# Tiled convolution: column pairs spread and further ahead, silu in halves, copies interleaved on ScalarE, a tile's rows in two parts on VectorE

## The reference

```python
f = fftshift(fft2(x))                                   # over rows and columns
amp, phase = abs(f), angle(f)
mod_amp = amp * sigmoid(amp @ w_h + b_h) + amp * sigmoid(amp @ w_l + b_l)
spatial = real(ifft2(ifftshift(mod_amp * exp(1j * phase))))
conv = conv3x3(spatial, w_f, padding='SAME') + b_f
y = silu(conv) + x
y = layernorm(y, over channels, eps=1e-3) * gamma + beta
```

## Time and profile before

| | us |
|---|---|
| runs, median (lowest to highest) | 4281.23 (4280.12 to 4282.1) |
| the profiled execution | 4282.0 |
| its span, first to last instruction | 4280.1 |
| PE busy in the span | 3983.8 (93%) |
| DVE busy | 3492.5 (82%) |
| ACT busy | 3194.4 (75%) |
| POOL busy | 2587.1 (60%) |
| start of the convolution stage of the four images (first column pair to last, L217) | 230.2 to 1654.5 |

### The profile page before, as it was taken

The page is one execution under the profiler, slowest core; times in us unless marked ns, Lnnn a source line. Parts: engine busy times, 40 slices in busy tenths (PEclk is TensorE's granted clock), DMA queues, the critical chain, the costliest instruction groups (busy, mean ns, idle before and its releaser), DMA issues.

```text
span 4280.1 us, 95150 instructions
## 1 busy us (share of the span) xinstructions
PE 3983.8 (93%) x31687; PEld 2863.5 (67%) x31687; DVE 3492.5 (82%) x8772; ACT 3194.4 (75%) x4968; POOL 2587.1 (60%) x2713
## 2 busy tenths in 40 slices
PE   7998898799979985799999999999999999999998
PEld 4787578757865885466666666666666666666665
DVE  4568447745775485699999999999999999999997
ACT  4445534553456354699999999999999999999997
POOL 0036103600460056588888888888888888888886
PEclk9999999999989998899999999999999999999999
DMA  2013101400140022111111111111111111111110
GB/s 91 1 53 129 57 2 63 156 20 11 63 164 3 11 72 81 38 41 38 42 39 42 39 42 39 42 39 42 39 39 40 39 42 39 42 39 42 39 42 26
DMA packets 214865, 205.93 MB, mean 48 GB/s; under 512 B 14368, under 2 KB 149152, under 8 KB 214688
## 3 DMA queue, kind: packets, MB, share of 16 engines
q1 hardware_dynamic: 214688, 203.60, 14.6%
HBM read 136.45 MB, written 67.11 MB: 48 GB/s over the span
## 4 chain that ended last, share of the span: by engine, by line
PE 58%; ACT 0%; DVE 0%; POOL 0%; issue 0%; POOLq 0%; DVEq 0%; ACTq 0%
PE g_ps L1043 7%; PE g_ps L1028 6%; PE g_ps L986 6%; PE g_ps L972 5%; PE g_ps L1031 5%; PE g_ps L1060 5%; PE g_ps L1003 3%; PE g_ps L1073 3%; PE g_ps L1079 3%; PE g_ps L1052 3%; PE g_ps L1012 3%; PE g_ps L977 3%; PE g_ps L992 2%; PE g_ps L1068 2%; PE g_ps L965 2%; PE g_ps L997 1%
## 5 line engine op out<-in xcount | busy, mean ns | idle before, releaser
L1355 DVE TENSOR_TENSOR g_mmat<-g_emat,g_ps 128x1024 f32<-128x1024 f32 x512 | 598.9, 1210 | 1.4 <-PE g_ps L1003 1.4
L1194 ACT ACTIVATE g_emat<-g_ps 128x1024 f32<-128x1024 f32 x512 | 521.1, 1024 | 85.7 <-PE g_ps L1031 84.2
L1298 DVE SCALAR_TENSOR_TENSOR g_acc<-g_ps,g_conv_w,g_acc 128x504 f32<-128x504 f32 (+1 forms) x768 | 554.5, 722 | 10.3 <-ACT g_acc L1157 9.9
L873 POOL TENSOR_TENSOR g_acc<-g_acc,g_tap 128x508 f32<-128x508 f32 x384 | 482.5, 1271 | 123.6 <-DVE g_acc L1298 123.6
L613 POOL MEMSET f_s_hi<- 128x192 f32 x4 | 1.0, 258 | 820.7 <-PE f_ps L344 820.7
L1043 PEld LDWEIGHTS g_ps<-g_mmat,g_dtx 128*32 128x32 f32 x8192 | 192.6, 109 | 310.6 <-issue 181.7
L1028 PE MATMUL g_ps<-g_rz,g_l 128*128 128x512 f32 x1024 | 390.0, 462 | 1.6 <-DVE g_z L1383 1.6
L229 PE MATMUL f_ps<-f_s_hi,f_wf_hi 128*128 128x256 f32 x1152 | 360.3, 313 | 5.0 <-DVE f_s_lo L466 5.0
L415 ACT ACTIVATE f_s_hi<-f_ps 128x384 fp32r<-128x384 f32 x256 | 125.7, 491 | 274.0 <-PE f_ps L217 268.9
L1043 PE MATMUL g_ps<-g_mmat,g_dtx 128*32 128x128 f32 x8192 | 329.2, 279 | 0.0
L230 PE MATMUL f_ps<-f_s_lo,f_wf_hi 128*128 128x256 f32 x1152 | 326.2, 283 | 0.0
(11 more groups left out here) (194 smaller groups left out, 12374.3 us busy)
## 6 DMA issues: line engine op xcount, KB each, us to landing
f_xt<-in_x_cols SPq DMA_DIRECT2D x32, 1024.0 KB, 10.3
f_xres<-in_x SPq DMA_DIRECT2D x128, 256.0 KB, 2.8
z<-f_zout SPq DMA_DIRECT2D x128, 256.0 KB, 2.0
g_zin<-z SPq DMA_DIRECT2D x128, 256.0 KB, 2.7
g_zres<-z SPq DMA_DIRECT2D x128, 256.0 KB, 2.9
out<-g_outb SPq DMA_DIRECT2D x128, 256.0 KB, 3.0
f_wf_raw<-in_w_f SPq DMA_DIRECT2D x1, 576.0 KB, 6.9
g_wx<-in_in_proj_t SPq DMA_DIRECT2D x1, 192.0 KB, 2.3
```

The costliest lines, as they stand in the source:

```text
L873: pool.tensor_tensor(acc[:, j, :, 1:], acc[:, j, :, 1:], tap1[:, j, :, 0:P - 1], ALU.add).then_inc(add_p[j], 1)
L1194: act.activation(emat[:, g, :].rearrange("p (b n) -> p b n", b=2), ps[:, D_BANK[g]:D_BANK[g] + 2, :], ACT.Exp).then_inc(e_a[g], 1)
L1298: dve.scalar_tensor_tensor(out=acc[:, j, :, k:], in0=four(ps[:, bank, :])[:, :, 0:P - k], scalar=conv_w[:, j, 3 - k:4 - k], in1=acc[:, j, ...
L1355: dve.tensor_tensor(mmat[:, g, :].rearrange("p (h n) -> p h n", h=HEADS), emat[:, g, :].rearrange("p (h n) -> p h n", h=HEADS), ps[:, CB, ...
```

## The change

- Seven column pairs, not five, are made ahead of tile 0 (AHEAD), in the banks 6, 7, 3, 4, 5, 0, 1. In `conv(k)` the pairs 4k+7 to 4k+10 follow the matmul groups 3, 7, 11 and 15 of 18 (a group is one shift of one position, three matmuls), so three are at least twelve matmuls apart; before they followed positions 0 to 3, nine apart.
- VectorE writes the rows without a step into a new buffer `rows_y` (a part of `work`), row by row; `tile_rows` is split. Its first part (L477 to L483) comes ahead of the last low part of the iteration, the second, `tile_ends` (L486 to L491), behind it. The first part also waits until silu of tile k-1 is done with `rows_y`.
- VectorE's iteration k is now: lo 4k+7, residual and moments (k-2, 0), lo 4k+8, residual and moments (k-2, 1), lo 4k+9, tile_rows(k), lo 4k+10, tile_ends(k).
- Silu reads `rows_y` and writes `conv_y`, two instructions of 512 elements a tile, with the step of 16 bytes now in its writes; it counts `silu_done` per half.
- ScalarE's iteration k is now: silu(k-1, 0), hi 4k+7, silu(k-1, 1), hi 4k+8, center(k-3, 0), hi 4k+9, middle(k), center(k-3, 1), hi 4k+10.
- The last three turned halves of an image use the banks 0, 1, 2 and not bank 7, and need not wait for each other's residual.

GpSimd and SP are unchanged. The core of the diff:

```diff
+AHEAD = 7
+HEAD_BANKS = (6, 7, 3, 4, 5, 0, 1)
+        rows_y = work[:, 3:5, :].rearrange("p a (b n) -> p (a b) n", b=2)
...
             def columns(b, u):
-                if u == 5:
-                    pe.wait_ge(lo_ready, b * UNITS + 1)
-                if u > 5:
-                    pe.wait_ge(lo_ready, b * UNITS + u)
-                bank = (6, 7, 3, 4, 5)[u] if u < 5 else 6
+                if u >= AHEAD:
+                    pe.wait_ge(lo_ready, b * UNITS + (1 if u == AHEAD else u))
+                bank = HEAD_BANKS[u] if u < AHEAD else 6
...
             def turn(b, k, h):
-                pe.wait_ge(silu_done, b * BATCHES + (k + 1))
-                pe.wait_ge(ysum_done, b * PARTS + (2 * k + h + 1))
+                pe.wait_ge(silu_done, b * PARTS + (2 * k + h + 1))
+                n = 2 * k + h
+                pe.wait_ge(ysum_done, b * PARTS + (min(n, 2 * BATCHES - 4) + 1))
+                bank = 7 if n <= 2 * BATCHES - 4 else n - 2 * BATCHES + 3
...
                 for n, p in enumerate((1, 3, 2, 4, 0, 5)):
-                    if n == 3 and k >= 2:
-                        turn(b, k - 2, 1)
-                    mm = position(k, p)
+                    for x in range(3):
+                        at = 3 * n + x
+                        if at == 9 and k >= 2:
+                            turn(b, k - 2, 1)
+                        mm = products(k, p, x)
+                        if at in (3, 7, 11, 15) and 4 * k + AHEAD + at // 4 < UNITS:
+                            columns(b, 4 * k + AHEAD + at // 4)
...
-                    if n < 4 and 4 * k + 5 + n < UNITS:
-                        columns(b, 4 * k + 5 + n)
...
-                def silu(k):
-                    act.wait_ge(y_done[k % 2], b * 8 + (k // 2 + 2))
-                    y = conv_y[:, k % 2].rearrange("p n i -> p (n i)")
-                    act.activation(y, y, ACT.Silu, bias=bias[:, 2:3]).then_inc(silu_done, 1)
+                def silu(k, h):
+                    if h == 0:
+                        act.wait_ge(y_done[k % 2], b * 8 + (k // 2 + 2))
+                    if k >= 2:
+                        act.wait_ge(vT_mm, b * PARTS + (2 * k - 3 + h))
+                    half = slice(4 * h * TILES, 4 * (h + 1) * TILES)
+                    act.activation(conv_y[:, k % 2, half].rearrange("p n i -> p i n"), rows_y[:, :, half], ACT.Silu,
+                                   bias=bias[:, 2:3]).then_inc(silu_done, 1)
...
                 for k in range(BATCHES + 3):
-                    for n in range(4):
-                        if 4 * k + 5 + n < UNITS:
-                            hi_part(4 * k + 5 + n)
-                        if n == 0 and 1 <= k <= BATCHES:
-                            silu(k - 1)
-                        if n in (1, 2) and k >= 3:
-                            center(k - 3, n - 1)
+                    if 1 <= k <= BATCHES:
+                        silu(k - 1, 0)
+                    if 4 * k + AHEAD < UNITS:
+                        hi_part(4 * k + AHEAD)
+                    if 1 <= k <= BATCHES:
+                        silu(k - 1, 1)
+                    if 4 * k + AHEAD + 1 < UNITS:
+                        hi_part(4 * k + AHEAD + 1)
+                    if k >= 3:
+                        center(k - 3, 0)
+                    if 4 * k + AHEAD + 2 < UNITS:
+                        hi_part(4 * k + AHEAD + 2)
                     if k < BATCHES:
                         middle(k)
+                    if k >= 3:
+                        center(k - 3, 1)
+                    if 4 * k + AHEAD + 3 < UNITS:
+                        hi_part(4 * k + AHEAD + 3)
...
                 dve.wait_ge(sum_done, done)
-                dve.scalar_tensor_tensor(out=y[:, :, 2], in0=sums[:, near], scalar=0.25, in1=sums[:, far],
+                if k:
+                    dve.wait_ge(silu_done, b * PARTS + 2 * k)
+                dve.scalar_tensor_tensor(out=rows_y[:, 2, :], in0=sums[:, near], scalar=0.25, in1=sums[:, far],
                                          op0=ALU.mult, op1=ALU.add)
...
+            def tile_ends(b, k):
...
-                dve.tensor_tensor(y[:, :, 0], ends[:, near], sums[:, far], ALU.add)
-                dve.tensor_tensor(y[:, :, 3], ends[:, far], diffs[:, far], ALU.add).then_inc(y_done[k % 2], 1)
+                dve.tensor_tensor(rows_y[:, 0, :], ends[:, near], sums[:, far], ALU.add)
+                dve.tensor_tensor(rows_y[:, 3, :], ends[:, far], diffs[:, far], ALU.add).then_inc(y_done[k % 2], 1)
...
                 for k in range(BATCHES + 2):
                     for n in range(4):
-                        if 4 * k + 5 + n < UNITS:
-                            lo_part(b, 4 * k + 5 + n)
-                        if n in (0, 2) and k >= 2:
-                            residual(b, k - 2, n // 2)
-                            moments(b, k - 2, n // 2)
+                        if n == 3 and k < BATCHES:
+                            tile_rows(b, k)
+                        if 4 * k + AHEAD + n < UNITS:
+                            lo_part(b, 4 * k + AHEAD + n)
+                        if n < 2 and k >= 2:
+                            residual(b, k - 2, n)
+                            moments(b, k - 2, n)
                     if k < BATCHES:
-                        tile_rows(b, k)
+                        tile_ends(b, k)
```

More of the change, by code:

```diff
@@ L219, in columns, with products @@
                 mm.then_inc(s_mm, 1)
-            def position(k, p):
+            def products(k, p, x):
                 at = 8 * k % RING
@@ L225, in position @@
                 out = ps[:, 3 * (k % 2) + bank, half * 256:half * 256 + 256].rearrange("p (w t) -> p w t", w=8)
[L226 to L232 removed]
+                hi = s_hi[:, at + x:at + x + 8, p * TILES:(p + 1) * TILES]
+                lo = s_lo[:, at + x:at + x + 8, p * TILES:(p + 1) * TILES]
+                pe.matmul(out, wf_hi[:, p, x, :], hi, start=(x == 0), stop=False)
+                pe.matmul(out, wf_hi[:, p, x, :], lo, start=False, stop=False)
+                return pe.matmul(out, wf_lo[:, p, x, :], hi, start=False, stop=(x == 2))
             def turn(b, k, h):
[L235 to L236 removed]
+                pe.wait_ge(silu_done, b * PARTS + (2 * k + h + 1))
+                n = 2 * k + h
+                pe.wait_ge(ysum_done, b * PARTS + (min(n, 2 * BATCHES - 4) + 1))
+                bank = 7 if n <= 2 * BATCHES - 4 else n - 2 * BATCHES + 3
                 y = conv_y[:, k % 2].rearrange("p n i -> p (n i)")
                 for r in range(4):
[L239 removed]
+                    mm = pe.transpose(ps[:, bank, r * P:(r + 1) * P], y[:, (4 * h + r) * P:(4 * h + r + 1) * P], ident[:, :])
                 mm.then_inc(vT_mm, 1)
             def conv(b, k):
[L243 removed]
+                pe.wait_ge(lo_ready, b * UNITS + (AHEAD if k == 0 else min(4 * k + 5, UNITS)))
                 pe.wait_ge(y_done[k % 2], b * 8 + (k // 2 + 1))
@@ L347, in _ @@
                     pe.wait_ge(t_free[j], b * 8 + 8)
-                for u in range(5):
+                for u in range(AHEAD):
                     columns(b, u)
@@ L409, in hi_part @@
                     act.wait_ge(s_mm, b * UNITS + (u + 1))
-                    at, bank = 2 * u % RING, (6, 7, 3, 4, 5)[u] if u < 5 else 6
+                    at, bank = 2 * u % RING, HEAD_BANKS[u] if u < AHEAD else 6
                     if at == 0 and u:
@@ L471, in tile_rows @@
                 done = b * BATCHES + (k + 1)
-                first, ends = ps[:, 3 * (k % 2), :], ps[:, 3 * (k % 2) + 2, :]
-                y = conv_y[:, k % 2]
+                first = ps[:, 3 * (k % 2), :]
                 near, far = slice(0, 256), slice(256, 512)
@@ L479, in tile_rows @@
                 dve.wait_ge(sum_done, done)
-                dve.scalar_tensor_tensor(out=y[:, :, 2], in0=sums[:, near], scalar=0.25, in1=sums[:, far],
+                if k:
+                    dve.wait_ge(silu_done, b * PARTS + 2 * k)
+                dve.scalar_tensor_tensor(out=rows_y[:, 2, :], in0=sums[:, near], scalar=0.25, in1=sums[:, far],
                                          op0=ALU.mult, op1=ALU.add)
                 dve.wait_ge(diff_done, done)
-                dve.scalar_tensor_tensor(out=y[:, :, 1], in0=diffs[:, near], scalar=0.5, in1=diffs[:, far],
+                dve.scalar_tensor_tensor(out=rows_y[:, 1, :], in0=diffs[:, near], scalar=0.5, in1=diffs[:, far],
                                          op0=ALU.mult, op1=ALU.add)
+            def tile_ends(b, k):
+                done = b * BATCHES + (k + 1)
+                ends = ps[:, 3 * (k % 2) + 2, :]
+                near, far = slice(0, 256), slice(256, 512)
                 dve.wait_ge(conv_mm, done)
@@ L498, in residual @@
                     dve.wait_ge(ln_done, b * PARTS + (n - 3))
-                dve.tensor_tensor(ysum[:, n % 4, :], ps[:, 7, :], xres[:, n % 4, :], ALU.add).then_inc(ysum_done, 1)
+                bank = 7 if n <= 2 * BATCHES - 4 else n - 2 * BATCHES + 3
```

(1 more changed line is left out.)

9 lines of the change are left out of this document (removed).

## The result

| | before | after |
|---|---|---|
| median, us | 4281.15 (4279.65 to 4282.1, 9 runs) | 4294.61 (4292.4 to 4303.1, 9 runs) |
| profiled execution, us (its span) | 4282.0 (4280.1) | 4293.05 (4290.7) |
| steady tile, us | 11.48 | 11.99 |
| last row instruction of tile 0 to that of tile 15, image 0, us | 173.48 | 176.15 |

The ratio is 1.0035, 95% interval 1.0025 to 1.0045. By the medians the kernel after is slower by 13.5 us, and all nine of its times lie above all nine of the kernel before. I had forecast 4292. Its times spread more (10.7 us against 2.5), and the two longest, 4300.24 and 4303.1, have the lowest mean granted clocks, 0.973 and 0.972 where the shortest have 0.974 and 0.975; no trace shows where in them the clock fell.

What follows compares the result with a forecast made beforehand. VectorE's loop through silu sets the tile: 10.87 plus 1.1 waiting for GpSimd, 11.97 against 11.48 us. Per image 5.4 - 2.0 - 0.6 = +2.8, four images +11 on the median 4281.2: 4292 us, range 4238 to 4346.

Steps and rivals of the forecast that it cites:

- the walk: Timing one steady tile instruction by instruction across the engines; it gave 10.87 us, 11.97 with VectorE's wait for GpSimd.
- zero: Start of a tile's first low part on VectorE (lo 4k+7), from which the forecast counted its times.
- The collision: VectorE's L480 just precedes GpSimd's second affine; L483 then waits for GpSimd on the shared port: 1.1 us more per tile.
- The silu half: ScalarE's 512-element silu instruction, slowed by its 16-byte write step and on VectorE's way: 0.88 us from start to start.
- The frame around the steady tile: Rest of an image: tiles 0 to 2 gain 2.0 us, tiles 14 and 15 gain 0.6 together with the last silu delay.
- the ring's wrap: Extra time where the hi, lo and columns ring wraps; an estimated 0.7 us, counted in tile 2.
- No collision: Rival, chance 0.35: GpSimd's affine starts later or the rows earlier, so neither row waits; tile 10.87 us, time 4244.
- Both rows wait: Rival, chance 0.25: GpSimd asks before L480, so L480 and L483 each wait; 2.3 us, tile 13.2, time 4345.
- the forecast's order: L480 starts at 6.63 us, GpSimd's second affine at 6.66 to 6.69, so VectorE's first row just wins the port.
- a new wait: VectorE, from L491 through silu half 0 and hi to the next low part: 1.91 us, of which its own slot is 0.34.

## Why the prediction held

**The bound and the walk.** VectorE's loop through silu sets the tile, as forecast: 11.99 against 11.97. Its steps, from zero: fourth low part 8.38 (8.4), L514 9.97 (10.05), then 2.01 (1.91). TensorE's wait on the low part is 1.47 + 0.29 = 1.76 per tile (2.0). Its own work is a little more than the 9.95 that I added up: the stalls of the kernel before are 0.74 and 0.69, 1.43 together and not 1.53.

**The collision** is a step without which the sign would have been the other, and it held with its size and its order: L497 0.42, L500 1.50. Removing the meeting gave 1.05 back, where the walk had 1.1. It isn't the only such step: without the silu half's step in its writes (0.9981), or with the hi first (0.9871), the change is a gain too. The reason for the turn-taking was read in one tile of the kernel before; eleven tiles of each image now show it.

**The silu half** is the term that was mis-sized: 0.88 from start to start, measured 1.01, near the top of the bounds of 0.49 to 1.05. I took it by analogy with VectorE, where the step adds 0.11 to 0.14 to 256 elements (from start to start, L490 0.45 in tile 15 of the kernel before, the former L490 now 0.34); on ScalarE it adds 0.38 to 512. Small errors the other way hid it: L514 to silu 0.45 for 0.51, and the last four instructions 1.59 for 1.64. The 11.97 was in part luck. The cacheline note of the Trainium skill ("SBUF — State Buffer", "Door 1: The DMA port swizzle") pointed the right way, and the run without the step agrees with it: 0.72 in place of 1.21.

**The frame around the steady tile** is less good than the total. The start of an image up to tile 2 gave 1.8 (forecast 2.0), tiles 14 and 15 gave 1.0 (1.3), and tiles 3 to 13 cost 4.7 (5.4). Of these I had set all eleven of the kernel before at 11.48 and all eleven of the kernel after at 11.97; they last 11.70 and 12.13 in the mean, mostly because I had put the ring's wrap into tile 2 alone, and tiles 6 and 10 have it too. The two errors nearly cancel. What follows the last tile costs 1.5, where I had 0.7 for the silu halves and took the rest as unchanged; this is the term of the frame that was most off. The first centering behind tile 15 starts 2.6 to 2.8 behind L514 where it was 1.7 behind L491: the two silu halves end 0.8 later than the single silu did, and in image 0 GpSimd's shift comes later still. The last group of centerings is 1.0 to 1.3 later; the rest lies in the transforms of the next image and differs from image to image. Together +3.4 per image against +2.8, so the total is right in part by errors of both signs.

**The rivals.** No collision: the run with GpSimd held back had tiles of 10.94 (the prediction's 10.87) and 4255 (4244). Both rows wait: in the kernel after it comes about in tiles 14 and 15, and in tile 14 GpSimd starts 0.44 ahead of L497:

```profile
410.01 1.13 DVE L497 SCALAR_TENSOR_TENSOR f_work<-f_work 128x256 f32<-128x256 f32 x1
411.07 1.50 DVE L500 SCALAR_TENSOR_TENSOR f_work<-f_work 128x256 f32<-128x256 f32 x1
...
409.57 1.29 POOL L657 TENSOR_TENSOR f_zout<-f_zout,f_gamma 128x512 f32<-128x512 f32 x1
```

It was given 0.25 because 0.03 to 0.06 us seemed to decide, and that is how near it was. In the kernel with five pairs ahead GpSimd won with a lead of 0.05 us, and VectorE won where GpSimd's lead was 0.01. In the kernel after VectorE is 0.05 ahead in the steady tiles, and in tiles 6 and 10 the two records start within 0.01 of each other and VectorE still wins. So the edge lies a few hundredths of a microsecond from the forecast's order. The order came out the same in all eleven tiles of all four images, but a walk of 6.6 us can't be right to hundredths but by luck. At that edge the price is the rival's: 1.2 us for the tile (15.67 against 14.43 and 14.46).

**What the prediction didn't see** is the largest thing in the study. It names the hi behind the silu half as a new wait and prices it, yet never compares it with the order that costs nothing to write: hi first. That is 1.45 us per tile, 66 us in all by the two medians (70 by the two ratios), five times the loss that was measured. Nor did it price what keeps TensorE's stalls short. No run tests the banks of the last three turned halves by themselves.

## What to carry over

When a copy that feeds a ring is placed behind an operation that waits for another engine's last result, price the wait for the other order too; the ring's copy was ready long before. When two engines share a port, look at when the uninvolved one starts: holding GpSimd back by 1.16 us was worth 1.05 us of each tile, though of the 12.5 us that an image's tiles gained 2.2 were lost again behind its last tile. And what "further ahead" is worth is read from the count that the consumer waits for: it was 1.08 us per tile, but only once the waits at the turn of the tile no longer covered it.

## What of the hardware was not expected

- TensorE's granted clock. In the 3 us behind stalls of 2.96 to 3.44 us (rows in one part) it was 0.50 to 0.58 in 22 cases and 1.00 in 12; behind stalls of 2.12 to 2.18 (and 2.57 to 2.65) it also did either. Behind the stalls of 1.95 it was 1.00 in all eight of the kernel after and fell in two of eight with the memset of 512 elements. Behind stalls of 1.47 in the kernel after it was always 1.00. The length of one stall doesn't decide; what does isn't shown. Where the clock falls, it costs some 1.4 us beside the stall.
- ScalarE's step. 512 elements written with a step of 16 bytes took 1.21 us, without it 0.72.
- The order on the shared port. By the records' starts, VectorE's row won with GpSimd 0.01 us ahead and lost with GpSimd 0.05 ahead (five pairs ahead); the loser waited for the whole operation.
- A memset of VectorE (0.11 and 0.48 us) did not wait for a running operation of GpSimd, but such an operation that had started 0.09 us ahead of it lasted 2.00 in place of 1.28.
